# A relational graph layer on one core: sixteen tiles of table rows that two queues fetch row by row go to GpSimd's gathers

## The reference

```python
h = jnp.maximum(_layernorm(x, axis=-1), 0.0)
W = jnp.einsum('rb,bio->rio', comp, basis)            # 64 relations, 64 x 64 each
msg = h[src] * weight
s = jax.ops.segment_sum(msg, etype * N + dst, num_segments=R * N).reshape(R, N, -1)
g = relu(jnp.einsum('rni,rio->no', s, W) + bias)      # one row per destination
y = g + relu(h @ res_w.T + res_b)
out = x + (y - mean(y, 0)) * rsqrt(var(y, 0) + 1e-5) * gamma + beta
```

## Time and profile before

| what | value |
|---|---|
| median of three timed executions | 1975.42 us |
| profiled execution's own time: its span (no other time of it is recorded) | 2559.4 us |
| GpSimd busy | 1474.2 us, 58% of the span |
| TensorE / VectorE / ScalarE busy | 1675.1 / 1040.2 / 1003.6 us |
| gathers of the head, of the table | 528, 1019 |
| DMAs of one row, SyncE's queue, ScalarE's queue | 1792, 256 |

### The profile page before, as it was taken

One profiled execution on the slowest core, in us unless ns is written; L12 is line 12 of the kernel. 1 busy time (PEld: TensorE's weight loads), 2 busy tenths in 40 slices (PEclk: granted clock), 3 DMA queues, 4 the chain that ended last, 5 costly groups with the idle time before them and its releaser, 6 DMA issues. The chain is left out here.

```text
span 2559.4 us, 29252 instructions
## 1 busy us (share of the span) xinstructions
PE 1675.1 (65%) x6522; PEld 817.4 (32%) x6571; DVE 1040.2 (41%) x3394; ACT 1003.6 (39%) x2898; POOL 1474.2 (58%) x1565
## 2 busy tenths in 40 slices
PE   1267677867787767466666677768778787872223
PEld 1222222323233222244444434434434343331112
DVE  0442013335233211255555535636546363632324
ACT  0255543424343332655555526526436252610001
POOL 7265535554465553366666666666666666666664
PEclk9997878878798878555555575575565757575656
DMA  7066667767687765111111111111111111111112
GB/s 141 24 244 264 263 250 275 304 234 285 254 341 300 291 230 198 45 42 40 43 40 40 43 28 41 42 27 39 40 31 39 31 40 31 35 23 41 39 41 63
DMA packets 120893, 308.66 MB, mean 121 GB/s; under 512 B 49361, under 2 KB 49644, under 8 KB 95395
## 3 DMA queue, kind: packets, MB, share of 16 engines
q1 hardware_dynamic: 56622, 233.21, 23.4%
q0 software_dynamic: 49504, 50.79, 10.6%
q10 hardware_dynamic: 14588, 22.76, 3.2%
HBM read 80.28 MB, written 226.35 MB: 120 GB/s over the span
## 5 line engine op out<-in xcount | busy, mean ns | idle before, releaser
L618 POOL DMA_INDIRECT shared<-z_table,idx_all x1019 | 967.3, 949 | 605.8 <-issue 233.6
L590 POOL DMA_INDIRECT acc<-in_x,idx_all x520 | 493.9, 950 | 448.5 <-DMA head_rows<-acc 299.7
L1238 PE MATMUL zps<-wp,res 128*128 128x512 bf16 x1915 | 503.3, 414 | 188.8 <-issue 79.9
L655 ACT ACTIVATE zst<-zps 128x512 f32<-128x512 f32 x480 | 276.9, 599 | 365.3 <-PE zps L1238 223.1
L762 ACT ACTIVATE res<-res,hw 128x64 f32<-128x64 f32 x1056 | 357.5, 426 | 104.2 <-issue 53.8
L1371 PE MATMUL mps<-wp,res 128*128 128x160 f32 (+4 forms) x528 | 271.9, 620 | 158.7 <-issue 84.4
L1238 PEld LDWEIGHTS zps<-wp,res 128*128 128x128 bf16 x1956 | 190.1, 103 | 490.6 <-issue 164.5
L1105 DVE TENSOR_SCALAR shared<-iota,rel_all,wgt_all 128x36 f32<-128x36 f32 (+9 forms) x1035 | 307.9, 326 | 62.0 <-ACT res L729 61.5
L1356 PE MATMUL zps<-shared 128*64 128x36 f32 (+9 forms) x1354 | 208.3, 317 | 146.2 <-issue 72.7
L749 ACT ACTIVATE res<-res,hm 128x64 f32<-128x64 f32 x528 | 176.0, 334 | 224.9 <-issue 132.2
L1356 PEld LDWEIGHTS zps<-shared 128*64 128x64 f32 x1354 | 143.7, 197 | 351.6 <-issue 283.3
(11 more groups left out here) (202 smaller groups left out, 1306.9 us busy)
## 6 DMA issues: line engine op xcount, KB each, us to landing
z_table<-zst SPq DMA_DIRECT2D x194, 1024.0 KB
wp<-z_table SPq DMA_DIRECT2D x1792, 0.2 KB
head_rows<-acc SPq DMA_DIRECT2D x66, 256.0 KB
res<-head_rows ACTq DMA_DIRECT2D x64, 256.0 KB
shared<-z_table,idx_all POOLq DMA_INDIRECT x1019
acc<-in_x,idx_all POOLq DMA_INDIRECT x520
wp<-z_table ACTq DMA_DIRECT2D x256, 0.2 KB
zst<-in_x ACTq DMA_DIRECT2D x12, 256.0 KB
```

Source lines behind the costliest of these rows:

```text
L590: e.indirect_dma_start(out=ring[:, b % NRING, i, :], out_offset=None, in_=x, in_offset=bass.IndirectOffsetOnAxis(ap=idx_first[:, t:t + 1] ...
L618: e.indirect_dma_start(out=ys[:, q % NY, :], out_offset=None, in_=table[:, :], in_offset=bass.IndirectOffsetOnAxis(ap=idx_all[:, col:col + ...
L655: e.activation(to, frm, ACT.Copy).then_inc(s_ez, 1)
L1238: last = e.matmul(to, lhsT=stationary(px, pw), rhs=moving(px, pw), start=(a == 0), stop=(a == 2))
```

## The change

The assignment of tiles to owners, `last_rows`, `fetch` and the buffers and semaphores for fetched rows go. GpSimd gathers all 1035 table tiles. The 13 loads of `x` move to SyncE's queue, which issues them in one go when the relations are summed. Shown without declarations:

```diff
-    owner, pooled, nsp, nact = {}, 0, 0, 0
-    for u, tiles in enumerate(units[:-NU]):
...
-    pool_tiles = [t for t in range(NZT) if t not in owner]
-        def fetch(e, t, r, to, landed):
...
@@ block.sync
-                table_landed(e)
-                e.wait_ge(s_met, 3)
-                for j, t in enumerate(sp_tiles):
-                    if j >= NSP:
-                        e.wait_ge(s_agg, sp_tiles[j - NSP] + 1)
-                    for r in range(P):
-                        fetch(e, t, r, sp_rows[:, j % NSP, :], s_sp[j % NSP])
+                e.wait_ge(s_rel, NHK)
+                for n in range(NEPI):
+                    load_x(e, n)
@@ block.gpsimd
-                for q, t in enumerate(pool_tiles):
+                for t in range(NZT):
                     col = seq[t][0]
-                    if q >= NY:
-                        e.wait_ge(s_agg, pool_tiles[q - NY] + 1)
-                    e.indirect_dma_start(out=ys[:, q % NY, :], ...
+                    if t >= NY:
+                        e.wait_ge(s_agg, t - NY + 1)
+                    e.indirect_dma_start(out=ys[:, t % NY, :], ...
@@ block.scalar
-                e.wait_ge(s_met, 3)
-                e.wait_ge(s_rel, NHK)
-                loaded = 0
-                for j, t in enumerate(act_tiles):
-                    for r in range(P):
-                        fetch(e, t, r, act_rows[:, j, :], s_act[j])
-                        if r % X_STEP == X_STEP - 1 and loaded < NEPI:
-                            load_x(e, loaded)
-                            loaded += 1
@@ block.vector, rows_of_table
-                e.tensor_scalar(last_rows[0:g, ch, :], idx_f[0:g, ch, GE - P:GE], float(ROW), None, ALU.mult).then_inc(s_met, 1)
@@ block.tensor
-                        if t in pool_nth:
...
+                        e.wait_ge(s_y[t % NY], 16 * (t // NY + 1))
+                        rows = ys[:, t % NY, :]
```

More of the change, by code:

```diff
@@ L62 @@
 ACT_TAKES = (9, 10)
[L66 to L69, removed]
 DVE_FROM = 24
@@ L158, in rgcn_kernel @@
     assert done == len(head_items)
-    owner, pooled, nsp, nact = {}, 0, 0, 0
-    for u, tiles in enumerate(units[:-NU]):
[L163 to L175, removed]
-    pool_tiles = [t for t in range(NZT) if t not in owner]
-    pool_nth = {t: q for q, t in enumerate(pool_tiles)}
-    ROW = 4 * F
     table = nc.dram_tensor("z_table", [NCLS * N * CLS, F], F32)
-    table_bytes = table[:, :].rearrange("(a n) f -> a (n f)", a=1).bitcast(U8)
     accd = nc.dram_tensor("acc_rows", [ROWS, F], F32)
@@ L221, in rgcn_kernel @@
         wp = sb("wp", [P, 3, R + 1, F], BF16)
-        fetched = wp[:, :, :, :].rearrange("p a r f -> p (a r f)").bitcast(F32)
-        sp_rows = fetched[:, 0:NSP * F].rearrange("p (s f) -> p s f", f=F)
-        act_rows = fetched[:, NSP * F:(NSP + ACT_TILES) * F].rearrange("p (s f) -> p s f", f=F)
+        wp_f = wp[:, :, :, :].rearrange("p a r f -> p (a r f)").bitcast(F32)
         HOH = max(HEAD_NODES) * HALF
-        hoh = fetched[:, (NSP + ACT_TILES) * F:(NSP + ACT_TILES) * F + NHOH * HOH].rearrange("p (s n) -> p s n", s=NHOH)
+        hoh = wp_f[:, 0:NHOH * HOH].rearrange("p (s n) -> p s n", s=NHOH)
         shared = sb("shared", [P, max(NY * F + NOH * WIN, 4 * BANK + 2 * LNT * F)])
@@ L250, in rgcn_kernel @@
         half_all = sb("half_all", [P, HEAD])
-        last_rows = sb("last_rows", [P, 2, P], I32)
         hsrc_i, hsrc_f = idx_all[:, HEAD:HEAD + HC * P], idx_all[:, HEAD:HEAD + HC * P].bitcast(F32)
@@ L326, in rgcn_kernel @@
         s_y = [sem(f"s_y{k}") for k in range(NY)]
-        s_sp = [sem(f"s_sp{k}") for k in range(NSP)]
-        s_act = [sem(f"s_act{k}") for k in range(ACT_TILES)]
         s_oh, s_agg, s_acc = sem("s_oh"), sem("s_agg"), sem("s_acc")
@@ L433, in fast_path_flag @@
             return e.value_load(flag_i[0:1, 0:1], min_val=0, max_val=1)
-        places = {}
-        def fetch(e, t, r, to, landed):
[L439 to L444, removed]
         def head_psum(t):
@@ L613, in _ @@
                 e.wait_ge(s_me, len(METAS))
-                for q, t in enumerate(pool_tiles):
+                for t in range(NZT):
                     col = seq[t][0]
-                    if q >= NY:
-                        e.wait_ge(s_agg, pool_tiles[q - NY] + 1)
-                    e.indirect_dma_start(out=ys[:, q % NY, :], out_offset=None, in_=table[:, :],
+                    if t >= NY:
+                        e.wait_ge(s_agg, t - NY + 1)
+                    e.indirect_dma_start(out=ys[:, t % NY, :], out_offset=None, in_=table[:, :],
                                          in_offset=bass.IndirectOffsetOnAxis(ap=idx_all[:, col:col + 1], axis=0)
-                                         ).then_inc(s_y[q % NY], 16)
+                                         ).then_inc(s_y[t % NY], 16)
             e.wait_ge(s_st, 7)
@@ L771, in _ @@
                             clear(sacc[:, a:a + 2048]).then_inc(s_flush, 1)
-                e.wait_ge(s_met, 3)
-                e.wait_ge(s_rel, NHK)
-                loaded = 0
-                for j, t in enumerate(act_tiles):
-                    for r in range(P):
-                        fetch(e, t, r, act_rows[:, j, :], s_act[j])
-                        if r % X_STEP == X_STEP - 1 and loaded < NEPI:
-                            load_x(e, loaded)
-                            loaded += 1
-                assert loaded == NEPI
             e.wait_ge(s_st, 3)
@@ L953, in rows_of_table @@
                 e.tensor_tensor(span, high, low, ALU.subtract)
-                link(e.scalar_tensor_tensor(out=idx_f[0:g, ch, :], in0=src_i[0:g, ch, :], scalar=float(R),
-                                            in1=ety_i[0:g, ch, :], op0=ALU.mult, op1=ALU.add))
-                e.tensor_scalar(last_rows[0:g, ch, :], idx_f[0:g, ch, GE - P:GE], float(ROW), None, ALU.mult).then_inc(s_met, 1)
+                e.scalar_tensor_tensor(out=idx_f[0:g, ch, :], in0=src_i[0:g, ch, :], scalar=float(R),
+                                       in1=ety_i[0:g, ch, :], op0=ALU.mult, op1=ALU.add).then_inc(s_met, 1)
             def take_meta(n):
```

## The result

The changed kernel takes 1997.61 us (median of four executions, 1994.7 to 1998.6) where the kernel before takes 1975.62 us. The ratio of the two, estimated from all executions, is 1.0102, with a 95% interval of 1.0090 to 1.0114: 20.2 us slower (17.8 to 22.5). The two medians by themselves are 22.0 us apart.

A forecast was written before the change was run, and what follows sets the result against it. The prediction took GpSimd's gathers to bound the timed kernel from end to end. Its terms, 20.0 - 0 + 0 + 0 = +20.0 us on 1975.4, gave 1995.4 us, 1.0% slower, range 1982 to 2002.

The forecast's parts named there:

- The bound: Whole kernel: GpSimd's gathers, 1547 at 1.25 us, bind the timed kernel from end to end.
- a floor of 1966.6 us: GpSimd's whole program: 4.3 us to first gather, 1933.8 us of gathers, 28.5 us at the end.
- The waits of the trace: Between gathers: 592.8 us of waits in the profiled execution, taken as stalls added by recording and refused.
- Rival A: Stage two up to tile 839: the head's work hides 11 added gathers, five cost 6.3 us, 1981.7 us; chance 0.09.
- Rival B: SyncE's fetched rows are late, so removing them makes it faster, 1948 us at 0.68 us a row; chance 0.06.
- Sixteen gathers, 20.0 us: Stage two, L618: sixteen gathers added to GpSimd's 1019, 1.25 us each, all on the path.
- Nothing hides it: GpSimd in stage two: none of the added gathers' time taken as hidden, at the most 8.8 us.
- the sign that I had named for the reading: TensorE waiting for `ys` in the last 200 tiles in both kernels would support the reading.
- The row fetches give back nothing: Removing 1792 row DMAs from SyncE's queue and 256 from ScalarE's: gain 0.
- my low end: SyncE's row fetches: 0.27 us a row, 35 us a tile, at which nothing waits.
- The loads of x: Thirteen loads moved from ScalarE's queue to SyncE's, after `s_rel`: cost 0, bounds 0 and 12 us.
- Rival C: The burst of loads on SyncE's queue lands on the gathers: 12 us more, 2007.4 us; chance 0.07.

The follow-up runs named there:

- the second trace: The kernel before, unchanged, profiled again on a slow chip: 2528.8 us against 2538.5 for its runs beside it, 0.997.
- the first trace: The kernel before, unchanged, in the profiled execution that the prediction read, on a slow chip: span 2559.4 us.
- the third: The kernel before, unchanged, profiled once more on a quick chip: 1976.7 us against 1977.2, 0.9995, span 1977.5.

## Why the prediction was right, and where it wasn't

**The bound.** Right for the chips that set the time. I had inferred from a floor of 1966.6 us, 8.8 us under the median, that GpSimd gathers without a pause. The quick trace of before shows it, and its account is 3.6 us, 527 steps of 1.261 us, 8.9 us to the first table gather, 1018 steps of 1.255 us, 23.2 us to the end. Two terms were off, one each way: a step is 1.255 to 1.261 us on average rather than 1.250 (+10.4 us over 1545 steps), and the end after the last gather is done is 22.3 us, not 28.5. The last was named as a possible 7 us. So it is in part luck that the sum lay within 0.5% of the timed median. With the terms of this trace the floor is 1969.8 us of its 1977.5.

**The waits of the trace.** Here a reason failed, though not the number. I wrote that the profiled execution was "the same program with stalls added by the recording". It was not the recording: unrecorded executions of the same kernel take as long on such a chip. Refusing the trace's waits was right because the time to be predicted came from a chip of the other kind. Had the comparison been made on a slow chip like that of the trace, the answer would have been no change, measured as 0.999, to which I gave 0.06. And it would have come by neither rival as I wrote them. By the medians sixteen gathers cost 24.6 us there, against A, and the fetched rows cost about as much. That is not B's lateness either, since in both slow traces of the kernel before TensorE waits for no fetched row. How the rows cost these 20.5 to 26.7 us stays open.

**Sixteen gathers, 20.0 us.** Right: 1.0102 is 20.2 us, and the dose fits on both sides. Eleven more gathers gave 13.5 us, four fewer -6.5, eight fewer -10.2; that is 1.23, 1.6 and 1.27 us each, with some 2.5 us of uncertainty in each total. The profiled spans differ by 15.3 us only, 1977.5 to 1992.8: 16 steps of 1.255 us are 20.1, and the first table gather came at 672.4 instead of 676.9, 4.5 us earlier. It came at 672.9 to 676.9 in the four quick traces of kernels with fetched rows, so most of this is likely the single execution's.

**Nothing hides it.** Right. I had 8.8 us as the most that could. Between the floor of the quick trace and its span lie 7.7 us, and all of them are the wait for the table, at the end of stage one as suspected. And TensorE waits for gathers in the last 200 tiles of both kernels, 92.9 us and 94.7 us in the two tables above: the sign that I had named for the reading.

**The row fetches give back nothing.** Right on a quick chip, by the traces: they never make TensorE wait. From one row to the next it is 0.32 us at the least, not the 0.27 of my low end, which I had read from a trace of a slow chip. A tile takes 51 us with its register loads, 0.40 us a row, where SyncE has 0.625. That the DMAs themselves don't slow the gathers is shown only by the gathers' pace, 1.255 us with and without them; the run with the sixteen tiles left out, meant for this, fell on slow chips twice, and there the rows cost 20.5 and 26.7 us by the medians. It was not measured on a quick one.

**The loads of x.** Right at 0. The changed kernel's timeline of SyncE, and a table of stretches (busy us and count of each engine, granted clock, DMA share, GB/s) around it:

```profile
1729.50 6.69 SPq L431 DMA_DIRECT2D zst<-in_x  x13
```

```profile
672.00:1735.00 1063.00, 926.89 (x3208) 491.00 (x3202) 660.23 (x2592) 613.27 (x2217) 805.03 (x846) 0.62 0.21 46
1735.00:1760.00 25.00, 10.57 (x44) 6.09 (x44) 6.30 (x28) 0.00 (x0) 18.88 (x20) 0.50 0.34 102
1760.00:1971.00 211.00, 99.19 (x386) 50.06 (x386) 62.06 (x222) 0.00 (x0) 159.67 (x169) 0.57 0.14 27
```

The thirteen loads are issued in 6.7 us and raise the DMA rate to 102 GB/s; in the same 25 us GpSimd makes 20 gathers, 1.25 us apart. Rival C's 12 us are nowhere in this trace.

**Rival A** was wrong on quick chips for the reason the floor gave. Up to 1735 TensorE is busy 926.9 us of 1063 in the changed kernel: 1.10 us a gather as in the earlier trace rows, and 0.15 us under GpSimd's pace is enough. **Rival B** was wrong there. On slow chips it is right for SyncE with 18 and with 22 tiles, and for the 14 of the kernel before it is not, though a row takes 0.755 us in the second trace and I had it decide from 0.665 on. That limit was worked out with gathers 1.25 us apart. In the second trace they are 1.488 us apart on average and SyncE starts 58.2 us after the first; with these the rows are in time up to (986 x 1.488 - 58.2) / 1792 = 0.79 us, an estimate.

The Trainium skill's rule in "DMA: Bandwidth & Descriptors", section "Issuing engines are not separate DMA queues", that other issuing engines save only the time of starting DMAs, holds in its mechanism. Its "usually small" does not hold here: that starting time, 1.255 us of GpSimd per gather beside a median of 2.4 us from issue to landing in the changed kernel's page, is the whole effect, with the DMA engines 14 to 34% busy in the stretches just shown.

## What to carry to other kernels

Count the instructions of each engine, multiply by their distance from start to start where nothing is waited for, and compare the sum with the timed median before trusting the share of busy time: here it was within half a percent while the busy shares named the wrong engine. When the profiled execution is much longer than the timed ones, look for which of the two the comparison will use; the constant distances carry over, the waits don't. A queue that takes work off the bounding engine pays by the instruction it saves as long as it has slack, and that slack should be read on the slowest chip the kernel may meet: with 22 tiles SyncE had it on a quick chip and not on a slow one.

## What the runs showed of the hardware

The same program takes 1976 us on some chips and 2540 us on others. GpSimd's gather of the table is the same on both, 948 to 951 ns, 1.25 us apart when undisturbed. What differs is the transport in stage one (about 400 GB/s against 230 to 340 in most slices) and the issue of small DMAs. In the second trace of before, on a slow chip, the row DMAs have these lengths, to be held against 227/228/324 above:

```profile
L444 SPq DMA_DIRECT2D wp<-z_table x1792: 2/197/1406, 1026.4 to 2378.3; - x200
```

The longest is 1.4 us, and the mean distance from row to row is 0.755 us with hardly a wait for a buffer, instead of 0.571 us of which 329.4 / 1791 = 0.18 are such waits. Behind the last of the head's work the engines stop for longer. VectorE's waits before L1088 for the next unit, over the last 240 to 250 us of gathers, are these in the first trace and then, the longest row of them, in the third, on a quick chip:

```profile
DVE acc L1088 <- remote: 157.2, 28, 11.7
```

```profile
DVE acc L1088 <- PE zps L1356: 107.1, 32, 5.9
```

TensorE stands for up to 11.6 us in that stretch of the first trace, while GpSimd starts 172 gathers in 250 us, 1.45 us each. It is not the row DMAs: in the changed kernel's trace from a slow chip VectorE stands for up to 17.8 us there. The traces of slow chips have no landing times of gathers, so whether these land late isn't shown. What causes it in those chips, or beside the kernel, stays open; none of these runs was built to tell. One consequence was measured: taking rows off GpSimd by SyncE with 22 tiles gains 0.5% on one kind and loses 13% on the other.
